# The weights of the product-key layers prepared inside the stage of memory gradients

## The reference

```python
x = x + memory(layernorm(x), Wk, Wv, Wq, Wout, W0, W1, gates)   # one gradient step on a small MLP, then read it
x = x + ffn(layernorm(x), gamma, beta, w_q, keys, key_in, key_out)
x = x + attention(layernorm(x), W_dq, W_uq, W_dkv, W_uk, W_uv, W_o)
x = x + ffn(layernorm(x), gamma, beta, w_q, keys, key_in, key_out)

# ffn: product-key experts, 8 heads, 64 x 64 = 4096 experts of width 256, batch norm over the tokens
q = (xn @ w_q.T) -> (side, head, 128);  sim = q . keys(head, 64, side, 128)      # two top-8s, then the best 8 of 64 pairs
o = gelu(x . key_in[idx]) * softmax(scores);  y = sum(o * key_out[idx])
```

## Time and profile before

| | before |
|---|---|
| median of 3 runs | 3795.75 us (3792.96 to 3796.88) |
| profiled execution | 3786.28 us |
| its span | 3784.5 us, mean granted TensorE clock 0.935 |
| busy in the span | PE 86%, PEld 60%, DVE 78%, ACT 42%, POOL 19% |

### The profile page before, as it was taken

One profiled execution on the slowest core, in us unless ns is written; L12 is line 12 of the kernel. 1 busy time (PEld: TensorE's weight loads), 2 busy tenths in 40 slices (PEclk: granted clock), 3 DMA queues, 4 the chain that ended last, 5 costly groups with the idle time before them and its releaser, 6 DMA issues. The chain is left out here.

```text
span 3784.5 us, 81506 instructions
## 1 busy us (share of the span) xinstructions
PE 3256.7 (86%) x29418; PEld 2271.4 (60%) x29418; DVE 2943.4 (78%) x8846; ACT 1597.5 (42%) x2173; POOL 708.5 (19%) x324
## 2 busy tenths in 40 slices
PE   4798379999999996559999999998468999999997
PEld 3587257787877775423334334333346877777786
DVE  3433599999999995548888788870579999999996
ACT  1211154444444431412666566666154444444441
POOL 0000033333333332020000000000023333333333
PEclk8799699999999998766999999999789999999999
DMA  6313700000000002693113333001810000000000
GB/s 214 107 47 96 235 9 10 13 16 19 11 19 10 19 10 63 215 183 47 24 32 52 51 52 52 6 6 34 265 49 4 15 19 10 19 10 19 13 13 15
DMA packets 203972, 198.98 MB, mean 53 GB/s; under 512 B 48246, under 2 KB 181686, under 8 KB 202166
## 3 DMA queue, kind: packets, MB, share of 16 engines
q1 hardware_dynamic: 203574, 193.65, 20.2%
HBM read 124.98 MB, written 68.22 MB: 51 GB/s over the span
## 5 line engine op out<-in xcount | busy, mean ns | idle before, releaser
L609 PE MATMUL f_p_route<-f_x_w,f_y_hot 128*128 128x64 f16 x8192 | 899.1, 193 | 81.9 <-DVE f_weighted L888 70.5
L622 PE MATMUL f_p_hid<-f_xtc,f_kin_t 128*128 128x256 f16 x6144 | 855.3, 273 | 25.4 <-issue 13.9
L633 PE MATMUL f_p_out<-f_kout,f_hidden 128*128 128x256 f16 x6144 | 856.0, 274 | 16.0 <-POOL f_hidden L531 15.9
L531 POOL TENSOR_TENSOR f_hidden<-f_weighted,f_hidden 128x1024 f16<-128x1024 f32 x256 | 609.9, 2383 | 1267.5 <-DVE f_x_w L878 1261.3
L1855 DVE TENSOR_REDUCE at_part_max<-at_p_ring 128x1 f32<-128x512 f32 (+3 forms) x1280 | 696.7, 603 | 138.3 <-PE at_p_ring L1721 71.9
L609 PEld LDWEIGHTS f_p_route<-f_x_w,f_y_hot 128*128 128x128 f16 x8192 | 691.4, 98 | 132.6 <-issue 107.0
L633 PEld LDWEIGHTS f_p_out<-f_kout,f_hidden 128*128 128x128 f16 x6144 | 602.4, 98 | 193.9 <-issue 118.6
L1838 ACT ACTIVATE at_prob<-at_p_s 128x1024 f32<-128x1024 f32 (+3 forms) x640 | 541.1, 895 | 294.4 <-PE at_p_s L1747 168.2
L622 PEld LDWEIGHTS f_p_hid<-f_xtc,f_kin_t 128*128 128x128 f16 x6144 | 599.8, 98 | 104.3 <-issue 26.9
L726 ACT CAST f_hidden<-f_weighted 128x1024 f16<-128x1024 f32 x256 | 343.1, 1340 | 525.2 <-DVE f_weighted L888 525.2
L721 ACT ACTIVATE f_hidden<-f_p_hid 128x512 f32<-128x512 f32 x512 | 301.1, 594 | 462.0 <-PE f_p_hid L622 460.9
(11 more groups left out here) (253 smaller groups left out, 3254.8 us busy)
## 6 DMA issues: line engine op xcount, KB each, us to landing
at_q<-qk SPq DMA_DIRECT2D x48, 256.0 KB, 15.4
at_k<-qk SPq DMA_DIRECT2D x48, 256.0 KB, 17.2
f_ln_xin<-x SPq DMA_DIRECT2D x16, 512.0 KB, 7.1
xt<-f_ln_xt SPq DMA_DIRECT2D x32, 256.0 KB, 5.2
f_kin_t<-kin_t SPq DMA_DIRECT2D x8, 1024.0 KB, 8.7
f_hidden<-in_L_ffn_key_out SPq DMA_DIRECT2D x8, 1024.0 KB, 6.9
f_xt_in<-xt SPq DMA_DIRECT2D x32, 256.0 KB, 2.8
f_xres<-x SPq DMA_DIRECT2D x32, 256.0 KB, 2.7
```

Of the source, the lines that this page charges most:

```text
L531: nc.gpsimd.tensor_tensor(lo, weighted[s % WR], hi, ALU.subtract).then_inc(lo_ready, 1)
L609: last = nc.tensor.matmul(p_route[:, t, :], y_hot[:, s % HR, t // PAIR, :, t % PAIR], x_w[:, s % HR, half, t // PAIR, :, t % PAIR], start= ...
L622: last = nc.tensor.matmul(p_hid[g % 2][:, xp % 2, :], kin_t[:, a, dh, xp * P:(xp + 1) * P], xt[slot][:, b, dh, :], start=i % 6 == 0, stop= ...
L633: last = nc.tensor.matmul(p_out[:, u, :], parts[slot][:, xp, u * P:(u + 1) * P, a], kout[:, b, xp, :], start=g == 0 and i == 0, stop=xp == ...
```

## The change

`product_key_prepare` shrinks to `identity_prepare`, which makes and stores only the identity. All else of it goes into `memory_gradients`, one piece to a step: item n (2 of keys, 4 of wct, 16 of key_in, in this order) is done by PE at the end of step n+4, and taken by ACT and DVE in step n+5. Beside these, key_out is split into its fp16 head and rest there (8 pieces of 128x1024, every third step, on ACT and DVE) and stored in a new DRAM tensor `kout_parts`. The two product-key stages load `kout` from it, and their ACT and POOL steps on key_out are gone. The loops of the stage are written out in full. 23 semaphores are added to the stage, 8 leave the first stage and 3 each of the product-key stages.

```diff
+def identity_prepare(nc, sem, ident_dram):
+            sp.wait_ge(ident_ready, ONE + 1)
             sp.dma_start(ident_dram, ident[:]).then_inc(stored, 16)
+            sp.wait_ge(stored, ONE + 16)
...
@@ load_weights, routed_experts @@
-                sp.dma_start(kout_rows[:, k, :], key_out.rearrange("(x y) d -> y x d", y=P)[:, k, :]).then_inc(kout_loaded, 16)
+                sp.dma_start(kout[:, :, k, :].rearrange("p a x d -> p a (x d)"),
+                             kout_dram[:, :, k, :].rearrange("p a x d -> p a (x d)")).then_inc(kout_loaded, 16)
...
-            for b in range(SHARES):
-                pool.wait_ge(kout_hi, ONE + b + 1)
-                nc.gpsimd.tensor_tensor(kout[:, 1, x, :], kout_rows[:, x, :], kout[:, 0, x, :], ALU.subtract).then_inc(kout_ready, 1)
...
-                nc.scalar.mul(kout_rows[:, x, :], kout_rows[:, x, :], E_SCALE).then_inc(kout_scaled, 1)
-                for g in range(2 * b, 2 * b + 2):
-                    gelu(0, 0, g)
-                act.wait_ge(kout_scaled, ONE + b + 1)
-                nc.scalar.copy(kout[:, 0, x, :], kout_rows[:, x, :]).then_inc(kout_hi, 1)
-                if b == 3:
+            for g in range(NG):
+                gelu(0, 0, g)
+                if g == NG // 2:
                     normalise(1)
                     copy_xt(1, 1)
...
@@ memory_gradients, SP @@
+            sp.dma_start(keyrows[:], keys.rearrange("h k s d -> (k s) h d")).then_inc(keys_loaded, 16)
+            sp.dma_start(wq[:], w_q.rearrange("(b k) d -> k b d", k=P)).then_inc(keys_loaded, 16)
+            for j in range(SLOTS):
+                load_kout(j)
+                load_kin(j)
+            for n in range(RING, NT + 3):
+                done = n - RING
+                if kout_item(done) is not None:
+                    store_kout(kout_item(done))
...
+                if kin_item(done) is not None:
+                    store_kin(kin_item(done))
...
+                if n < NT:
+                    load(n, n % RING)
@@ memory_gradients, PE, ACT and DVE @@
+            def prepare(n):
+                above(pe, prep_taken, n)
...
+                    for x in range(XG):
+                        last = nc.tensor.transpose(p_prep[:, x * P:(x + 1) * P], kin[j % SLOTS][:, x, dh * P:(dh + 1) * P], ident[:])
+                last.then_inc(prep_ready, 1)
...
+                if 4 <= n < 4 + N_PREP:
+                    prepare(n - 4)
...
+                    act.wait_ge(prep_ready, ONE + n + 1)
+                    above(act, kin_stored[i % SLOTS], i // SLOTS * 16)
+                    nc.scalar.mul(kin_parts[i % SLOTS][:, 0, :], p_prep[:], E_SCALE).then_inc(kin_hi, 1)
...
+                    dve.wait_ge(kin_hi, ONE + i + 1)
+                    nc.vector.scalar_tensor_tensor(kin_parts[i % SLOTS][:, 1, :], p_prep[:], E_SCALE, kin_parts[i % SLOTS][:, 0, :],
+                                                   ALU.mult, ALU.subtract).then_inc(prep_taken, 1)
```

More of the change, by code:

```diff
@@ L235 @@
 E_SCALE = 16.0
-def product_key_prepare(nc, sem, ident_dram, w_q, keys, key_in, wct_dram, kin_dram):
+def identity_prepare(nc, sem, ident_dram):
     with ExitStack() as ctx:
[L243 to L262, removed]
+        ident = ctx.enter_context(nc.sbuf_tensor("ip_ident", [P, P], F32))
+        ident_zero, ident_ready, stored = sem("ip_ident_zero"), sem("ip_ident_ready"), sem("ip_stored")
         block = ctx.enter_context(nc.Block())
@@ L1067, in _, with load_kin @@
-            for m in range(RING):
-                load(0, m)
-            with sp.Fori(1, NT // RING) as i:
-                for m in range(RING):
-                    load(i, m)
+                    sp.dma_start(xt[m][:, h, :], xt_dram[n // 2, :, h, (n % 2) * P:(n % 2 + 1) * P]).then_inc(s["xt_loaded"][m], 16)
+                sp.dma_start(xln[m][:], xln_dram[n * P:(n + 1) * P, :]).then_inc(s["xln_loaded"][m], 16)
+            def load_kin(j):
+                above(sp, prep_taken, FIRST_KIN + DH * (j - SLOTS + 1) if j >= SLOTS else 0)
+                sp.dma_start(kin[j % SLOTS][:], key_in.rearrange("(x y) d -> y x d", y=P)[:, j * XG:(j + 1) * XG, :]).then_inc(
+                    kin_loaded[j % SLOTS], 16)
@@ L1078, in step @@
+            def step(n, m):
                 m1, m2, m3 = (m - 1) % RING, (m - 2) % RING, (m - 3) % RING
@@ L1113, in step @@
                 if valid(n - 3):
-                    first, end = isinstance(n, int) and n == 3, isinstance(n, int) and n == NT + 2
-                    pe.wait_ge(s["xln_loaded"][m3], ONE + ((it if m >= 3 else it - 1) * 16 + 16))
+                    first, end = n == 3, n == NT + 2
+                    pe.wait_ge(s["xln_loaded"][m3], ONE + (n - 3) // RING * 16 + 16)
                     pe.wait_ge(s["d1_ready"], ONE + n - 2)
@@ L2095, in hybrid_block @@
     with StageSemaphores(nc) as sem:
-        product_key_memory(nc, sem, "f2_", x3, y, xt, ident, wct, kin, f("key_out"), f("gamma"), f("beta"))
+        product_key_memory(nc, sem, "f2_", x3, y, xt, ident, wct, kin, kout, f("gamma"), f("beta"))
 def kernel(**inputs):
```

232 lines of the change are left out of this document (122 added, 110 removed).

## The result

The changed kernel takes 3771.5 us (median of 5 runs, 3767.4 to 3776.2), the kernel before 3793.9 in the same comparison (5 runs, 3788.5 to 3796.9): ratio 0.9945, 95% interval 0.9933 to 0.9956. The prediction was 3755 us with a range from 3743 to 3769. The sign was right and the size was not: 22.4 us were gained by the medians, 18.9 by the two profiled executions (3786.3 and 3767.4 us), where 40.6 were forecast.

A forecast was written before the change was run, and what follows sets the result against it. Bounds: a first stage running alone, PE in the gradients, ACT and PE in turn in the prologues. -49.4 + 14.9 + 1.35 - 0.35 + 0.1 - 7.2 = -40.6 us gave 3745.7 profiled, 3755 unprofiled; range 3743 to 3769.

The forecast's parts named there:

- First stage: Start of the program: only the identity and its store remain, next stage starts at 4.8 us instead of 54.23, -49.4 us.
- Stage of gradients: memory_gradients: PE has no gap, so moved transposes (7.9 us) and wct matmuls (7.0) cost their full time, +14.9 us.
- rival of pieces that wait: Stage of gradients: late DVE, wct at its old pace or first loads hold PE, +6 to +13 us; chance 0.17.
- Semaphores: Ahead of the stage of gradients: SP increments 23 more semaphores at 0.058 us each while PE waits, +1.35 us.
- Prologues: Both product-key stages before their rounds: without ACT's scaling and cast PE sets the pace, 3.6 us each, -7.2 us.
- its last condition: Rounds of the product-key stages: the prediction would be wrong if these, left as they are, took another time.

The follow-up runs named there:

- experiment 10: Changed kernel with 36 more PE instructions at its start, each of the 64 key_in transposes in the stage of gradients done twice: 3760.1 us, ratio 0.9916.
- experiment 9: Changed kernel with 36 more PE instructions at its start, key_out's halves made in the product-key stages again: 3756.8 us, ratio 0.991.
- experiment 12: Changed kernel with rounds written out, early load of f_xt_in and 36 PE instructions, key_out's halves made in the product-key stages again: 3745.5 us, ratio 0.9875.
- experiments 3, 5 and 6: In order: kernel before, 90 more PE instructions ahead of second stage's rounds, 3805.1 us; changed kernel, 36 more at start, 3751.2; kernel before, 220 more, 3805.7.
- experiment 8: Changed kernel with 36 more PE instructions at its start and the load of f_xt_in issued early: 3750.2 us, ratio 0.99.
- experiment 3: Kernel before with 90 more PE instructions ahead of the second product-key stage's rounds: 3805.1 us, ratio 1.0035.
- experiment 2: Changed kernel with 160 more PE instructions ahead of the second product-key stage's rounds: 3773.3 us, ratio 0.9949.

## Why the prediction was right and wrong

**First stage** (-49.4): right, -49.8.

**Stage of gradients** (+14.9): right in size and reason, +14.5. The choice that carried it, transposes and wct matmuls at 0.11 us as PE's upper level, holds by the timeline; experiment 10 measures it with 64 more, 7.0 us. The rival of pieces that wait didn't occur. For wct no row had shown the upper level; the piece at 118.51 us does, 0.109 us each. The ten traces with the pieces done once have 206.1 to 207.4 us for the stage, so +14.5 to +15.8. The wct matmuls last 273 ns at the median there (experiment 10 shows the same rows), where the earlier trace rows had 415.

**Semaphores** (+1.35): ACT's table load to mg_ident took 3.28 us instead of 1.93, so +1.35.

**Prologues** (-7.2): right in sign and reason, and in size as far as the traces can tell: -9.3 between the two traces, 6.1 by experiment 9, 9.5 by experiment 12. The mean from f_ident to the first store is 172.3 and 172.9 us in the five traces with the conversion there and 168.9 and 168.5 in the nine without, 7.8 us together.

**The step that failed** is one that the prediction named only as its last condition: "the rounds of the product-key stages, which the change leaves as they are". It stood in the sum as a term of nothing, and had no rival and no chance. They took 7.1 and 11.4 us more, 18.5 of the 21.7 us by which the two profiled executions miss the forecast of -40.6. The instructions of the rounds are the same, but the changed kernel has another amount of PE code ahead of them, which moves the loop against its 16 KB blocks. In the first product-key stage a packet of instructions then falls into the load of f_xt_in; in the second PE stops a second time 12 matmuls behind the loop's first instruction, for up to 2.3 us, as if a block ended there, and at three turns the granted clock falls behind the stop. Shown by: 36 PE instructions that do nothing give the time back (0.9903 instead of 0.9945), 220 in the kernel before make it lose as much (1.004) with nothing moved, and the early load and the written-out loop take away one symptom and both. -37.7 us remain of the change when the place is put right; -40.6 was forecast.

Smaller things were not in the sum either. Of the +2.8 us ahead of the stage of gradients 1.35 are semaphores; the rest is no more than executions differ by, since the same kernel again had +1.1 (74.0 us). The +2.1 us of update, read and normalisation was +0.2 in the run again. The +2.2 of attention was +5.8 there and +1.4 with the 36 instructions, so no cause can be read from it.

What stays argued only: that the packet delays the load by sharing one of the DMA engines with it. The traces show that both coincide: of 60 loads on every other chunk (before, changed, experiments 3, 5 and 6) the 16 with a packet 1.3 to 1.5 us behind their issue landed after 3.85 to 4.12 us, the other 44 after 2.51 to 3.25. The experiments show that the packet's place decides. Which DMA engine carried it was not looked at. That the second stop is a wait for the next block is argued too, from the place of the packets and from the missing semaphore; the profile names no releaser.

## What to carry to other kernels

A change in one stage moves the code of all later ones. Where later stages are hardware loops that PE fills to 95%, a shift of some tens of instructions was worth 15 to 18 us of the rounds here, nearly as much as the change's own net gain; before a gain or loss under 1% is put down to an edit, compare stages that the edit doesn't touch, and look for waits that end by issue and for the landing of short loads. Two cures were tried: to write out a short hot loop (here 16 chunks; the inner ones took 59.7 us each without exception), and to issue a load ahead of a store that waits, so that no small delay of it counts.

## What the runs showed of the hardware

- A turn of the rounds' loop, with 2714 PE instructions in the trace, costs PE a stop that no semaphore explains: 1.07 to 1.43 us at the turns shown, and 2.26 us more at the turn of the changed kernel's second stage, where a packet comes right behind the loop's first instruction. Ten turns written out gave 11.4 us in the rounds over experiment 8.
- Not every turn costs: in the kernel before, the loop of the stage of gradients, about 510 PE instructions, had no packet from 212 to 302 us, no wait of PE and steps of 5.62 us throughout.
- Short stops can cost twice: at three of five turns of the changed kernel's second stage, behind stops like those of 1.07 and 2.26 us, the granted clock stood at its lower level for about 3.4 us, and such a chunk took 2 us more than those of the other two turns.
- One instruction packet of 16 KB within the load of 256 KB went with a landing of 3.9 instead of 2.8 us.
- A wait on PE for a semaphore that has long been met is not free: between gamma's load and f_ident lie 12.4 us with 90 of these instructions (experiment 3) and 19.3 with 160 (experiment 2), so about 0.1 us each.
